# Local attention in six layers: exponentials scaled by the queries' norm, odd heads normalised on GpSimd, another order on TensorE

## The chip, the cores and the metric

The kernel runs on one core of a Trainium2 chip. Its engines run side by side and meet through semaphores: PE (TensorE, matrix products, with PEld for its weight loads), DVE (VectorE), ACT (ScalarE), POOL (GpSimd), and SP, which issues transfers. The metric is the device time of one execution in microseconds, lower is better.

## The reference

A chain of conditional layers and feed-forward layers over `x` of 32 sequences x 128 tokens x 128 features. The change is in the attention of "L2_ffn", which is done six times (`DEPTH`), each time followed by a feed-forward layer:

```python
def attn_layer(x, Wqkv, qs, ksc, Wo):        # x: (32, 128, 128), 16 heads of 64
    q, k, v = heads(x @ Wqkv)
    q = l2norm(q) * qs
    k = l2norm(k) * ksc
    q = q * cos * scale + rotate_half(q) * sin * scale
    k = k * cos / scale + rotate_half(k) * sin / scale
    return heads_back(local_attention(q, k, v)) @ Wo

def local_attention(q, k, v):                # windows of 32: this one and the one before
    sim = einsum('bhwie,bhwje->bhwij', q, k) * 8.0
    sim = where(mask, -finfo.max, sim)
    return einsum('bhwij,bhwje->bhwie', softmax(sim), v)
```

`l2norm(t)` is `t` over its norm within a head. The queries' norm is one number for each token and head, so it can be put on q or on the row of scores.

## The kernel before

`level2_layers` holds the six layers; the other functions stand before and after it and aren't touched. A unit is one sequence and 8 of its 16 heads, so a layer has 32 x 2 = 64 units. Tokens lie on the 128 partitions. The heads of a unit are split by e = 0 (even) and e = 1 (odd): the scores of four heads of 128 x 128 fill one PSUM bank, and `s_ps` has two.

Each engine has its own program. `pipeline(engine, units, period, stages)` writes it: in slot s it calls every stage `(f, g)` of the list for unit s - g, in the order of the list. Eight slots are written out in a loop body (8 times round a layer, less head and tail). The list's order is the order of the engine's queue: what stands behind a waiting instruction waits too. VectorE's slots run one slot number ahead (its list has `rotate` with lag 1 where PE's has `project_k` with lag 0).

What a unit k passes through:

- PE: `project_q` (L1509) and `project_k` (L1512) write q and k, 2 x 512 columns, to `qk_ps`; `project_v` (L1518) writes v to `vy_ps`.
- VectorE: `rotate` (L1860) and `rotate_swapped` (L1866) multiply q and k from PSUM with the rotary tables into `t1` and `t2`. ScalarE: `squares` (L1695) writes `sq` out of `qk_ps`. VectorE: `sums` adds up the squares of a head into `ss` (L1874) and takes the maximum with `tiny` (L1877).
- GpSimd, `norms`: t1 = t1 + t2 (L1798), rs = ss to the power of -1/2 (L1800), qk = t1 x rs for q and k alike (L1805).
- PE: `turn_q` (L1525) and `turn_k` (L1531) transpose four tiles each into `T_ps`; ScalarE copies them with `keep_q` (L1706) and `keep_k` (L1712). As there is one `T_ps`, `turn_k` waits for `keep_q`, and the next `turn_q` for `keep_k`.
- PE, `scores`: a product of the mask (L1541, bf16) and then q by k (L1546) into both banks of `s_ps`; it waits for `kTc` (the copy of k), `p0` and `p1` of the unit before, as the banks are read until then. The tables of q carry the factor -8, and the mask's product is +2^100 where a key may not be seen: `s_ps` holds the negated scores.
- VectorE, `lows`: the minimum of each row and head (L1888), one reduction for each e, each with its own semaphore `low0` or `low1`.
- ScalarE, `exps0` and `exps1` (L1718): four exponentials each, in place, bias `low`, scale -1.0, each with its row sum into `den` (a second instruction, ACTIVATION_READ_ACCUMULATOR).
- VectorE, `normalise0` and `normalise1`: reciprocal of `den` (L1894), then p = s_ps x rec (L1897).
- PE: `turn_p0` and `turn_p1` (L1552), ScalarE `keep_p0` and `keep_p1` (L1732), PE `values` (L1573), ScalarE `keep_o` (L1744), PE `project` (L1584), VectorE `residual` (L1910). `keep_v` (L1701) copies v. `shift` (L1853, L1854), once for two units, prepares the input `xs`.

The orders of the four engines:

```python
pe:   (turn_q,2) (project_q,0) (turn_p1,4) (turn_k,2) (project_k,0)
      (values,4) (turn_p0,3) (project_v,0) (scores,2) (project,4)
act:  (keep_q,2) (keep_p1,4) (exps1,3) (keep_k,2) (keep_o,4) (keep_p0,3)
      (keep_v,0) (squares,0) (exps0,2)
dve:  (normalise0,4) (shift,0) (rotate,1) (normalise1,4) (rotate_swapped,1)
      (lows,3) (sums,1) (residual,5)
pool: norms
```

After 64 units the feed-forward layer follows (`ffn`), on the same engines; its first steps are laced into the last slots (`before`, `after`).

Of the kernel before, what the change touches and what calls it, by code (L numbers as in the profile page):

```python
# [24 lines left out]
P = 128  # L25
# [15 lines left out]
UH = 8  # L41
# [1367 lines left out]
def level2_layers(nc, T, R):  # L1409
# [8 lines left out]
    with ExitStack() as ctx:  # L1418
# [13 lines left out]
        rs = m.sb("rs", [P, 2, 2 * UH])  # L1432
        t1 = m.sb("t1", [P, 2, 2 * UC])
        t2 = m.sb("t2", [P, 2, 2 * UC])
        qk = m.sb("qk", [P, 2, 2 * UC])
        qT = m.sb("qT", [P, 2, 4, P])
        kT = m.sb("kT", [P, 2, 4, P])
        low = m.sb("low", [P, 2, 2, 4])
        den = m.sb("den", [P, 2, 2, 4])
# [31 lines left out]
        names = ("tables", "one", "xs", "qkp", "vp", "vc", "sq", "ss", "ssm", "rs", "t1", "t2", "t12", "qk", "qT",  # L1471
                 "qTc", "kT", "kTc", "scores", "low0", "low1", "ex0", "ex1", "rec0", "rec1", "p0", "p1", "pT0", "pT1",
# [6 lines left out]
        with nc.Block() as block:  # L1479
# [24 lines left out]
            def _(pe):  # L1504
# [16 lines left out]
                def turn_q(k, j, c):  # L1521
                    pe.wait_ge(s_["qk"], at(k))
                    pe.wait_ge(s_["kTc"], at(k - 1))
                    for i in range(4):
                        mm = pe.transpose(T_ps[:, i * P:(i + 1) * P], qk[:, c % 2, i * P:(i + 1) * P], R.ident[:, :])  # L1525
                    mm.then_inc(s_["qT"], 1)

                def turn_k(k, j, c):
                    pe.wait_ge(s_["qTc"], at(k))
                    for i in range(4):  # L1530
                        mm = pe.transpose(T_ps[:, i * P:(i + 1) * P], qk[:, c % 2, UC + i * P:UC + (i + 1) * P],  # L1531
                                          R.ident[:, :])
                    mm.then_inc(s_["kT"], 1)

                def scores(k, j, c):
                    pe.wait_ge(s_["kTc"], at(k))
                    pe.wait_ge(s_["p0"], at(k - 1))
                    pe.wait_ge(s_["p1"], at(k - 1))
# [68 lines left out]
                def spread(l, j):  # L1607
# [5 lines left out]
                    if j == 1:  # L1613
                        pe.wait_ge(s_["p1"], at(l * NU + NU - 1))
# [66 lines left out]
                with pe.Fori(0, DEPTH) as l:  # L1681
                    pe.wait_ge(s_["f_res"], at(l * NG - 1))
                    pipeline(pe, NU, 8, [(turn_q, 2), (project_q, 0), (turn_p1, 4), (turn_k, 2), (project_k, 0),
                                         (values, 4), (turn_p0, 3), (project_v, 0), (scores, 2), (project, 4)],
# [6 lines left out]
            def _(act):  # L1691
# [23 lines left out]
                def exps(k, c, e):  # L1715
                    act.wait_ge(s_[f"low{e}"], at(k))
                    for i in range(4):
                        ins = act.activation(s_ps[:, e, i * P:(i + 1) * P], s_ps[:, e, i * P:(i + 1) * P], ACT.Exp,  # L1718
                                             bias=low[:, c % 2, e, i:i + 1], scale=-1.0,
# [54 lines left out]
                with act.Fori(0, DEPTH) as l:  # L1774
                    pipeline(act, NU, 8, [(keep_q, 2), (keep_p1, 4), (exps1, 3), (keep_k, 2), (keep_o, 4), (keep_p0, 3),
# [1057 lines left out]
```

## Time and profile before

| | us |
|---|---|
| median of 3 runs | 5947.21 |
| lowest, highest | 5918.96, 5953.5 |
| span of the profiled execution | 5933.1 |

The profiled execution's own time isn't listed apart from the runs; its span, from the first to the last instruction, is 14 us under the median. The profile is one execution on the chip. Its first part says how long each engine was busy:

```profile
PE 5194.6 (88%) x43284; PEld 3252.2 (55%) x43296; DVE 3850.6 (65%) x6824; ACT 3367.5 (57%) x9898; POOL 3172.7 (53%) x1509
```

The second part cuts the span into 40 slices and gives busy tenths:

```profile
PE   5994999456599999999999999999999899996864
DVE  2112000752388868886788768886888588856888
ACT  0000000432188957996689759884899499943432
POOL 0000000221388848885688758884888388841018
PEclk9999999668699999999999999999999999997985
```

A digit 9 is 90% or more. The six layers lie in slices 11 to 35, from 1.6 to 5.3 ms; a dip of POOL is a feed-forward layer. A timeline row has the start, the duration, engine and line, output and inputs, the count of instructions merged, and in brackets the idle time ahead of it and what ended it.

### The profile page before, as it was taken

The page shows a single profiled execution, that of the slowest core. Times are in us where ns is not written, and L with a number is a line of the kernel's source. Part 1 is how long each engine was busy: PE and PEld are TensorE (multiplying, and loading weights), DVE is VectorE, ACT ScalarE, POOL GpSimd, SP SyncE. Part 2 cuts the span into 40 slices and gives each one's busy share as a digit, 9 for nine tenths or more (in the row PEclk, how much of TensorE's full clock was granted, in tenths as well). Part 3 has the DMA queues.
Part 4 walks back from the last instruction along what each step waited for, and adds up shares of the span by engine and source line. Part 5 has one row for each costly group of instructions (what it writes and reads, how often), then busy time and mean ns, then how long its engine had stood idle before and what let it go on. Part 6 is the DMA issues. An engine that isn't in the chain of part 4 may idle for free. (4 is left out here: it accounts for less than half of the span.)

```text
span 5933.1 us, 128823 instructions
## 1 busy us (share of the span) xinstructions
PE 5194.6 (88%) x43284; PEld 3252.2 (55%) x43296; DVE 3850.6 (65%) x6824; ACT 3367.5 (57%) x9898; POOL 3172.7 (53%) x1509
## 2 busy tenths in 40 slices
PE   5994999456599999999999999999999899996864
PEld 1331776233366655666566656664666466654532
DVE  2112000752388868886788768886888588856888
ACT  0000000432188957996689759884899499943432
POOL 0000000221388848885688758884888388841018
PEclk9999999668699999999999999999999999997985
DMA  7666554021100000000000000000000000000000
GB/s 227 162 171 156 111 108 101 4 69 47 34 1 0 0 16 5 0 0 16 5 0 0 15 5 0 0 0 20 1 0 0 20 1 0 0 16 13 7 1 14
DMA packets 271956, 199.78 MB, mean 34 GB/s; under 512 B 179032, under 2 KB 254264, under 8 KB 265336
## 3 DMA queue, kind: packets, MB, share of 16 engines
q1 hardware_dynamic: 202073, 119.60, 8.6%
q10 hardware_dynamic: 67487, 71.25, 4.1%
q8 instruction: 229, 3.75, 0.3%
q0 software_dynamic: 2048, 4.20, 0.2%
q14 instruction: 119, 0.97, 0.1%
HBM read 131.83 MB, written 63.16 MB: 33 GB/s over the span
## 5 line engine op out<-in xcount | busy, mean ns | idle before, releaser
L1800 POOL TENSOR_TENSOR rs<-ss,minus_half 128x16 f32<-128x16 f32 x386 | 1127.4, 2921 | 282.3 <-DVE ss L1877 281.5
L1718 ACT ACTIVATE s_ps<-s_ps,low 128x128 f32<-128x128 f32 x3072 | 1050.0, 343 | 81.5 <-DVE low L1888 76.2
L1798 POOL TENSOR_TENSOR t<-t 128x1024 f32<-128x1024 f32 x386 | 909.2, 2356 | 151.9 <-DVE t L1866 151.0
L1805 POOL TENSOR_TENSOR qk<-t,rs 128x1024 f32<-128x1024 f32 x386 | 734.4, 1903 | 60.5 <-POOL rs L1800 23.7
L1718 ACT ACTIVATION_READ_ACCUMULATOR s_ps<-s_ps,low 128x1 f32 x3072 | 641.8, 209 | 0.0
L1888 DVE TENSOR_REDUCE low<-s_ps 128x4 f32<-128x512 f32 x768 | 494.9, 686 | 203.5 <-PE s_ps L1546 203.4
L1860 DVE TENSOR_TENSOR t<-qk_ps,rot 128x1024 f32<-128x1024 f32 x386 | 472.5, 1224 | 162.1 <-PE qk_ps L1512 148.2
L1897 DVE TENSOR_TENSOR p<-s_ps,rec 128x512 f32<-128x512 f32 x768 | 531.0, 691 | 30.5
L1552 PEld LDWEIGHTS pT_ps<-ident,p 128*128 128x128 f32 x3072 | 354.7, 141 | 267.8 <-issue 265.5
L264 PE MATMUL h_ps<-h_x,h_w 9*128 9x512 bf16 x4096 | 439.9, 628 | 69.2 <-DMA h_w<-rows_w1s 54.5
L1732 ACT ACTIVATE pT<-pT_ps 128x512 f32<-128x512 f32 x768 | 459.5, 598 | 64.7 <-PE pT_ps L1552 29.8
L1573 PEld LDWEIGHTS att_oT_ps<-pT,v 128*64 128x64 f32 x6144 | 330.7, 137 | 287.0 <-issue 287.0
L1552 PE MATMUL pT_ps<-ident,p 128*128 128x128 f32 x3072 | 485.0, 281 | 0.8
L1695 ACT ACTIVATE sq<-qk_ps 128x1024 f32<-128x1024 f32 x386 | 395.0, 1023 | 145.9 <-DVE t L1866 114.1
L1874 DVE TENSOR_REDUCE ss<-sq 128x16 f32<-128x1024 f32 x386 | 466.8, 1209 | 4.8 <-ACT sq L1695 4.8
L1866 DVE TENSOR_TENSOR t<-qk_ps,rot 128x1024 f32<-128x1024 f32 x386 | 468.7, 1214 | 0.0
L1584 PE MATMUL vy_ps<-oT,wo 128*128 128x128 f32 x3072 | 447.8, 289 | 4.4 <-ACT oT L1744 4.4
L1573 PE MATMUL att_oT_ps<-pT,v 128*64 128x128 f32 x6144 | 423.7, 280 | 8.8 <-issue 8.8
L1509 PE MATMUL qk_ps<-wqkv,xs 128*128 128x512 f32 x772 | 403.4, 605 | 31.6 <-DVE xs L1854 20.2
L1518 PE MATMUL vy_ps<-wqkv,xs 128*128 128x512 f32 x768 | 400.3, 603 | 29.6 <-ACT v L1701 15.5
L1546 PEld LDWEIGHTS s_ps<-kT,qT 64*128 64x128 f32 x6144 | 407.5, 189 | 9.1
L1546 PE MATMUL s_ps<-kT,qT 64*128 64x128 f32 x6144 | 405.7, 272 | 0.0
(404 smaller groups left out, 8703.6 us busy)
## 6 DMA issues: line engine op xcount, KB each, us to landing
h_x<-rows_xs SPq DMA_DIRECT2D x512, 72.0 KB
rows_hs<-h_parts ACTq DMA_DIRECT2D x88, 384.0 KB, 6.8
z_fm<-rows_hs SPq DMA_DIRECT2D x128, 144.0 KB
x_fm<-rows_hs SPq DMA_DIRECT2D x128, 144.0 KB
wqkv<-in_wqkv SPq DMA_DIRECT2D x7, 1536.0 KB, 6.4
o_w<-rows_exs ACTq DMA_DIRECT2D x512, 18.0 KB
rows_xs<-z_fm ACTq DMA_DIRECT2D x12, 384.0 KB, 5.5
rows_exs<-s_exp ACTq DMA_DIRECT2D x9, 512.0 KB, 6.5
```

Source lines behind the costliest of these rows:

```text
L1546: mm = pe.matmul(s_ps[:, e, i * P:(i + 1) * P], qT[r, c % 2, i, :], kT[r, c % 2, i, :], start=False, stop=True, skip_group_check=True)
L1552: mm = pe.transpose(pT_ps[:, i * P:(i + 1) * P], p[:, c % 2, e, i, :], R.ident[:, :])
L1573: mm = pe.matmul(oT_ps[DH * e:DH * e + DH, i * P:(i + 1) * P], v[:, c % 8, d:d + DH], pT[:, c % 2, e, i, :], start=True, stop=True, skip_g ...
L1718: ins = act.activation(s_ps[:, e, i * P:(i + 1) * P], s_ps[:, e, i * P:(i + 1) * P], ACT.Exp, bias=low[:, c % 2, e, i:i + 1], scale=-1.0, ...
L1798: pool.tensor_tensor(t1[:, i, :], t1[:, i, :], t2[:, i, :], ALU.add).then_inc(s_["t12"], 1)
L1800: pool.tensor_tensor(rs[:, i, :], ss[:, i, :], R.minus_half[:, 0:2 * UH], ALU.pow).then_inc(s_["rs"], 1)
L1805: pool.tensor_tensor(qk[:, i, :].rearrange("p (h d) -> p h d", d=DH), t1[:, i, :].rearrange("p (h d) -> p h d", d=DH), rs[:, i, :].unsquee ...
L1860: dve.tensor_tensor(t1[:, i, :], qk_ps[:, :, :].rearrange("p n c -> p (n c)"), rot[:, 0, :, :, :].rearrange("p a h d -> p (a h d)"), ALU.m ...
L1866: dve.tensor_tensor(t2[:, i, :].rearrange("p (h e d) -> p h e d", e=2, d=DH // 2), swapped(), rot[:, 1, :, :, :].rearrange("p a h (e d) -> ...
L1874: dve.tensor_reduce(ss[:, i, :], sq[:, :].rearrange("p (h d) -> p h d", d=DH), AX.X, ALU.add).then_inc(s_["ss"], 1)
L1888: dve.tensor_reduce(low[:, c % 2, e, :], s_ps[:, e, :].rearrange("p (h k) -> p h k", h=4), AX.X, ALU.min).then_inc(s_[f"low{e}"], 1)
L1897: dve.tensor_tensor(p[:, i, e, :, :], s_ps[:, e, :].rearrange("p (h k) -> p h k", h=4), rec[:, i, e, :].unsqueeze(2).to_broadcast([P, 4, P ...
```

## The change

What it does, in `level2_layers` and the constants:

- The signs are turned: the tables of q carry +8, the mask -2^100, and `s_ps` holds scores.
- q is no longer multiplied with its `rs`: `turn_q` transposes `t1` and waits for `t12` (the addition) alone. Only k is multiplied, into `kn` (half the size). `rs` has four buffers instead of two, as it is used longer.
- `lows` takes the maxima of both e into `top`, waits for them, and writes `low` = -top x rs for all eight heads in one instruction. There is one semaphore `low` for both halves.
- `exps` takes `rs` of its head as scale (a [128,1] operand) instead of the constant -1.0. `exps1` writes to `grown` in SBUF, `exps0` stays in place in PSUM.
- p of the odd heads is made by GpSimd out of `grown` (`normalise1`, before the `norms` of the unit three later); VectorE keeps its reciprocal (`invert1`).
- `scores` waits for `ex1` instead of `p1` of the unit before.
- PE's order: `project_k` between `turn_p1` and `turn_k`, then `project_v`, `values`, `scores`, `turn_p0`, `project`. ScalarE's order: `keep_v` ahead of `keep_o`, then `squares`, `keep_p0`.

```diff
--- before.py
+++ after.py
@@ -1429,13 +1429,15 @@
...
         ss = m.sb("ss", [P, 2, 2 * UH])
-        rs = m.sb("rs", [P, 2, 2 * UH])
+        rs = m.sb("rs", [P, 4, 2 * UH])
...
         t2 = m.sb("t2", [P, 2, 2 * UC])
-        qk = m.sb("qk", [P, 2, 2 * UC])
+        kn = m.sb("kn", [P, 2, UC])
...
         kT = m.sb("kT", [P, 2, 4, P])
+        top = m.sb("att_top", [P, 2, 2, 4])
         low = m.sb("low", [P, 2, 2, 4])
+        grown = m.sb("grown", [P, 2, 4, P])
...
@@ -1519,23 +1521,23 @@
...
                 def turn_q(k, j, c):
-                    pe.wait_ge(s_["qk"], at(k))
+                    pe.wait_ge(s_["t12"], at(k))
...
                     for i in range(4):
-                        mm = pe.transpose(T_ps[:, i * P:(i + 1) * P], qk[:, c % 2, i * P:(i + 1) * P], R.ident[:, :])
+                        mm = pe.transpose(T_ps[:, i * P:(i + 1) * P], t1[:, c % 2, i * P:(i + 1) * P], R.ident[:, :])
...
                 def turn_k(k, j, c):
                     pe.wait_ge(s_["qTc"], at(k))
+                    pe.wait_ge(s_["kn"], at(k))
                     for i in range(4):
-                        mm = pe.transpose(T_ps[:, i * P:(i + 1) * P], qk[:, c % 2, UC + i * P:UC + (i + 1) * P],
-                                          R.ident[:, :])
+                        mm = pe.transpose(T_ps[:, i * P:(i + 1) * P], kn[:, c % 2, i * P:(i + 1) * P], R.ident[:, :])
...
                 def scores(k, j, c):
...
                     pe.wait_ge(s_["p0"], at(k - 1))
-                    pe.wait_ge(s_["p1"], at(k - 1))
+                    pe.wait_ge(s_["ex1"], at(k - 1))
...
@@ -1611,7 +1613,7 @@
...
                     if j == 1:
-                        pe.wait_ge(s_["p1"], at(l * NU + NU - 1))
+                        pe.wait_ge(s_["ex1"], at(l * NU + NU - 1))
...
@@ -1680,8 +1682,8 @@
...
                     pe.wait_ge(s_["f_res"], at(l * NG - 1))
-                    pipeline(pe, NU, 8, [(turn_q, 2), (project_q, 0), (turn_p1, 4), (turn_k, 2), (project_k, 0),
-                                         (values, 4), (turn_p0, 3), (project_v, 0), (scores, 2), (project, 4)],
+                    pipeline(pe, NU, 8, [(turn_q, 2), (project_q, 0), (turn_p1, 4), (project_k, 0), (turn_k, 2),
+                                         (project_v, 0), (values, 4), (scores, 2), (turn_p0, 3), (project, 4)],
...
@@ -1713,10 +1715,14 @@
...
                 def exps(k, c, e):
-                    act.wait_ge(s_[f"low{e}"], at(k))
+                    act.wait_ge(s_["low"], at(k))
+                    if e:
+                        act.wait_ge(s_["p1"], at(k - 2))
                     for i in range(4):
-                        ins = act.activation(s_ps[:, e, i * P:(i + 1) * P], s_ps[:, e, i * P:(i + 1) * P], ACT.Exp,
-                                             bias=low[:, c % 2, e, i:i + 1], scale=-1.0,
+                        h = 2 * i + e
+                        raw = s_ps[:, e, i * P:(i + 1) * P]
+                        ins = act.activation(grown[:, c % 2, i, :] if e else raw, raw, ACT.Exp,
+                                             bias=low[:, c % 2, e, i:i + 1], scale=rs[:, c % 4, h:h + 1],
...
@@ -1772,8 +1778,8 @@
...
                 with act.Fori(0, DEPTH) as l:
-                    pipeline(act, NU, 8, [(keep_q, 2), (keep_p1, 4), (exps1, 3), (keep_k, 2), (keep_o, 4), (keep_p0, 3),
-                                          (keep_v, 0), (squares, 0), (exps0, 2)], k0=l * NU, last=lambda i: after(l, i),
+                    pipeline(act, NU, 8, [(keep_q, 2), (keep_p1, 4), (exps1, 3), (keep_k, 2), (keep_v, 0), (keep_o, 4),
+                                          (squares, 0), (keep_p0, 3), (exps0, 2)], k0=l * NU, last=lambda i: after(l, i),
...
@@ -1797,15 +1803,16 @@
...
                     pool.wait_ge(s_["ssm"], at(k))
-                    pool.tensor_tensor(rs[:, i, :], ss[:, i, :], R.minus_half[:, 0:2 * UH], ALU.pow
+                    pool.wait_ge(s_["ex1"], at(k - 4))
+                    pool.tensor_tensor(rs[:, c % 4, :], ss[:, i, :], R.minus_half[:, 0:2 * UH], ALU.pow
...
                     pool.wait_ge(s_["kT"], at(k - 2))
-                    pool.tensor_tensor(qk[:, i, :].rearrange("p (h d) -> p h d", d=DH),
-                                       t1[:, i, :].rearrange("p (h d) -> p h d", d=DH),
-                                       rs[:, i, :].unsqueeze(2).to_broadcast([P, 2 * UH, DH]), ALU.mult
-                                       ).then_inc(s_["qk"], 1)
+                    pool.tensor_tensor(kn[:, i, :].rearrange("p (h d) -> p h d", d=DH),
+                                       t1[:, i, UC:2 * UC].rearrange("p (h d) -> p h d", d=DH),
+                                       rs[:, c % 4, UH:2 * UH].unsqueeze(2).to_broadcast([P, UH, DH]), ALU.mult
+                                       ).then_inc(s_["kn"], 1)
...
@@ -1817,14 +1824,27 @@
...
 
+                def normalise1(k, c):
+                    i = c % 2
+                    pool.wait_ge(s_["rec1"], at(k))
+                    pool.wait_ge(s_["pT1"], at(k - 2))
+                    pool.tensor_tensor(p[:, i, 1, :, :], grown[:, i, :, :],
+                                       rec[:, i, 1, :].unsqueeze(2).to_broadcast([P, 4, P]), ALU.mult
+                                       ).then_inc(s_["p1"], 1)
+
...
                     for u in range(2, 8):
+                        if u >= 3:
+                            normalise1(l * NU + u - 3, u - 3)
...
                         for u in range(8):
+                            normalise1(l * NU + 5 + i * 8 + u, (u + 5) % 8)
                             norms(l * NU + 8 + i * 8 + u, 8 + i * 8 + u, u)
+                    for u in range(NU - 3, NU):
+                        normalise1(l * NU + u, u % 8)
...
@@ -1856,7 +1876,8 @@
                 def rotate(k, j, c):
...
                     dve.wait_ge(s_["qkp"], at(k))
-                    dve.wait_ge(s_["qk"], at(k - 2))
+                    dve.wait_ge(s_["qT"], at(k - 2))
+                    dve.wait_ge(s_["kn"], at(k - 2))
...
@@ -1885,24 +1906,30 @@
...
                         dve.wait_ge(s_[f"rec{e}"], at(k - 2))
-                        dve.tensor_reduce(low[:, c % 2, e, :], s_ps[:, e, :].rearrange("p (h k) -> p h k", h=4), AX.X,
-                                          ALU.min).then_inc(s_[f"low{e}"], 1)
-
-                def normalise(k, c, e):
+                        ins = dve.tensor_reduce(top[:, c % 2, e, :], s_ps[:, e, :].rearrange("p (h k) -> p h k", h=4),
+                                                AX.X, ALU.max)
+                    ins.then_inc(s_["top"], 1)
+                    dve.wait_ge(s_["top"], at(k))
+                    dve.wait_ge(s_["rs"], at(k))
+                    dve.scalar_tensor_tensor(low[:, c % 2, :, :], top[:, c % 2, :, :], -1.0,
+                                             rs[:, c % 4, 0:UH].rearrange("p (i e) -> p e i", e=2), ALU.mult, ALU.mult
+                                             ).then_inc(s_["low"], 1)
+
+                def normalise0(k, j, c):
                     i = c % 2
-                    dve.wait_ge(s_[f"ex{e}"], at(k))
-                    dve.reciprocal(rec[:, i, e, :], den[:, i, e, :]).then_inc(s_[f"rec{e}"], 1)
-                    dve.wait_ge(s_[f"rec{e}"], at(k))
-                    dve.wait_ge(s_[f"pT{e}"], at(k - 2))
-                    dve.tensor_tensor(p[:, i, e, :, :], s_ps[:, e, :].rearrange("p (h k) -> p h k", h=4),
-                                      rec[:, i, e, :].unsqueeze(2).to_broadcast([P, 4, P]), ALU.mult
-                                      ).then_inc(s_[f"p{e}"], 1)
-
-                def normalise0(k, j, c):
-                    normalise(k, c, 0)
-
-                def normalise1(k, j, c):
-                    normalise(k, c, 1)
+                    dve.wait_ge(s_["ex0"], at(k))
+                    dve.reciprocal(rec[:, i, 0, :], den[:, i, 0, :]).then_inc(s_["rec0"], 1)
+                    dve.wait_ge(s_["rec0"], at(k))
+                    dve.wait_ge(s_["pT0"], at(k - 2))
+                    dve.tensor_tensor(p[:, i, 0, :, :], s_ps[:, 0, :].rearrange("p (h k) -> p h k", h=4),
+                                      rec[:, i, 0, :].unsqueeze(2).to_broadcast([P, 4, P]), ALU.mult
+                                      ).then_inc(s_["p0"], 1)
+
+                def invert1(k, j, c):
+                    i = c % 2
+                    dve.wait_ge(s_["ex1"], at(k))
+                    dve.wait_ge(s_["p1"], at(k - 2))
+                    dve.reciprocal(rec[:, i, 1, :], den[:, i, 1, :]).then_inc(s_["rec1"], 1)
...
@@ -2002,7 +2029,7 @@
...
                 with dve.Fori(0, DEPTH) as l:
-                    pipeline(dve, NU, 8, [(normalise0, 4), (shift, 0), (rotate, 1), (normalise1, 4), (rotate_swapped, 1), (lows, 3),
+                    pipeline(dve, NU, 8, [(normalise0, 4), (shift, 0), (rotate, 1), (invert1, 4), (rotate_swapped, 1), (lows, 3),
...
@@ -2711,7 +2738,7 @@
...
     out = np.empty((S, 2, 2, DH), np.float32)
-    out[:, 0, 0], out[:, 0, 1] = np.cos(freqs) * scale * -8, np.sin(freqs) * scale * sign * -8
+    out[:, 0, 0], out[:, 0, 1] = np.cos(freqs) * scale * 8, np.sin(freqs) * scale * sign * 8
...
@@ -2738,7 +2765,7 @@
...
     b[38:42] = (block[None, :] > w[:, None]) | (block[None, :] < w[:, None] - 1)
-    return np.concatenate([a, a]), np.concatenate([b, b]) * 2.0 ** 100
+    return np.concatenate([a, a]), np.concatenate([b, b]) * -2.0 ** 100
 def constants():
```

## Rows read from the trace of the kernel before

**Rows 1.** Engines by stretch: one slot (us, busy and count by engine, clock).

```profile
2405.44:2413.46 8.02, 8.02 (x66) 5.42 (x65) 6.79 (x12) 7.26 (x24) 7.12 (x4) 1.00 0.00 0
```

**Rows 2.** Timeline, PE, first half of that slot.

```profile
2405.44 0.60 PE L1525 MATMUL T_ps<-ident,qk 128*128 128x128 f32 x4
...
2405.88 1.02 PE L1509 MATMUL qk_ps<-wqkv,xs 128*128 128x512 f32 x2
...
2406.74 0.60 PE L1552 MATMUL pT_ps<-ident,p 128*128 128x128 f32 x4
...
2407.34 0.66 PE L1531 MATMUL T_ps<-ident,qk 128*128 128x128 f32 x4
...
2407.83 1.02 PE L1512 MATMUL qk_ps<-wqkv,xs 128*128 128x512 f32 x2
...
2408.78 1.09 PE L1573 MATMUL att_oT_ps<-pT,v 128*64 128x128 f32 x16
```

**Rows 3.** Timeline, VectorE and GpSimd, one slot.

```profile
2402.82 1.22 DVE L1866 TENSOR_TENSOR t<-qk_ps,rot 128x1024 f32<-128x1024 f32 x1
...
2405.77 1.21 DVE L1874 TENSOR_REDUCE ss<-sq 128x16 f32<-128x1024 f32 x1
...
2407.02 0.17 DVE L1877 TENSOR_TENSOR ss<-ss,tiny 128x16 f32<-128x16 f32 x1
...
2407.27 2.91 POOL L1800 TENSOR_TENSOR rs<-ss,minus_half 128x16 f32<-128x16 f32 x1 [0.76 <-DVE ss L1877]
...
2410.31 1.90 POOL L1805 TENSOR_TENSOR qk<-t,rs 128x1024 f32<-128x1024 f32 x1
...
2412.17 2.36 POOL L1798 TENSOR_TENSOR t<-t 128x1024 f32<-128x1024 f32 x1
```

**Rows 4.** Timeline, ScalarE, the same slot.

```profile
2406.67 0.61 ACT L1706 ACTIVATE qT<-T_ps 128x512 f32<-128x512 f32 x1
...
2407.37 0.60 ACT L1732 ACTIVATE pT<-pT_ps 128x512 f32<-128x512 f32 x1
...
2407.87 0.34 ACT L1718 ACTIVATE s_ps<-s_ps,low 128x128 f32<-128x128 f32 x1
...
2409.23 0.62 ACT L1712 ACTIVATE kT<-T_ps 128x512 f32<-128x512 f32 x1
```

**Rows 5.** Groups by shape: busy us, mean ns of one, idle before.

```profile
L714 ACT ACTIVATE big<-st_ps,magic,sc 128x512 f32<-128x512 f32 x32 | 24.7, 773 | 40.4 <-DVE inv L653 40.4
...
L1753 ACT ACTIVATE ff_sq<-qk_ps 128x512 f32<-128x512 f32 x48 | 28.6, 597 | 0.0
...
L1816 POOL TENSOR_TENSOR ff_diag<-ident,ff_rstd 128x512 f32<-128x512 f32 x48 | 49.9, 1039 | 75.5 <-PE s_ps L1615 74.5
```

**Rows 6.** Timeline, VectorE, around a mask product that waited for p.

```profile
2418.67 0.69 DVE L1897 TENSOR_TENSOR p<-s_ps,rec 128x512 f32<-128x512 f32 x1
...
2420.91 1.29 DVE L1888 TENSOR_REDUCE low<-s_ps 128x4 f32<-128x512 f32 x2 [0.42 <-PE s_ps L1546]
```

**Rows 7.** Timeline, VectorE instructions that began inside one of GpSimd.

```profile
2237.76 2.34 POOL L1798 TENSOR_TENSOR t<-t 128x1024 f32<-128x1024 f32 x1
...
2239.83 0.31 DVE L1877 TENSOR_TENSOR ss<-ss,tiny 128x16 f32<-128x16 f32 x1
...
2243.34 1.90 POOL L1805 TENSOR_TENSOR qk<-t,rs 128x1024 f32<-128x1024 f32 x1 [0.22 <-POOL rs L1800]
...
2243.42 1.97 DVE L1853 SCALAR_TENSOR_TENSOR xs<-z_fm 64x128 f32<-64x128 f32 x1 [3.28 <-issue]
...
2415.29 2.91 POOL L1800 TENSOR_TENSOR rs<-ss,minus_half 128x16 f32<-128x16 f32 x1 [0.76 <-DVE ss L1877]
...
2416.72 0.27 DVE L1853 SCALAR_TENSOR_TENSOR xs<-z_fm 64x128 f32 x1
```

**Rows 8.** Timeline, GpSimd, units 2 and 63 of the first layer.

```profile
1630.59 2.35 POOL L1798 TENSOR_TENSOR t<-t 128x1024 f32<-128x1024 f32 x1 [3.56 <-DVE t L1866]
...
2121.84 2.36 POOL L1798 TENSOR_TENSOR t<-t 128x1024 f32<-128x1024 f32 x1 [0.39 <-DVE t L1866]
```

More of the change, by code:

```diff
@@ L1470, in level2_layers @@
         ffw = m.dma_sem("e_ffw")
-        names = ("tables", "one", "xs", "qkp", "vp", "vc", "sq", "ss", "ssm", "rs", "t1", "t2", "t12", "qk", "qT",
-                 "qTc", "kT", "kTc", "scores", "low0", "low1", "ex0", "ex1", "rec0", "rec1", "p0", "p1", "pT0", "pT1",
+        names = ("tables", "one", "xs", "qkp", "vp", "vc", "sq", "ss", "ssm", "rs", "t1", "t2", "t12", "kn", "qT",
+                 "qTc", "kT", "kTc", "scores", "top", "low", "ex0", "ex1", "rec0", "rec1", "p0", "p1", "pT0", "pT1",
                  "pTc0", "pTc1", "o", "oTc", "proj", "res",
```

## The prediction

> **What bounds the kernel now.** I read the page first, then a table of engines over one stretch, then the timeline of one slot engine by engine, then the groups by shape. The page's busy shares (PE 88%) are an average over stages. The six attention layers fill 3.6 ms of the span, and the change lies in them alone. A layer handles 64 units; in a slot each engine does its stages for several units. GpSimd starts its addition (L1798) for unit 2 at 1630.59 and for unit 63 at 2121.84 [rows 8]: 61 slots in 491.25 us, 8.05 each. In one slot PE is busy 8.02 of 8.02 us [rows 1], and its groups follow each other without a gap [rows 2]: PE bounds the slot. The reader is to see that the groups cost more than their columns: four transposes take 0.44 us up to the next start behind `project` (L1525), but 0.60 ahead of `turn_k`, which waits for ScalarE's copy of q, and 0.49 ahead of `project_k`; a projection takes 0.86 ahead of a transpose and 0.95 ahead of `values`, whose weights are 64 columns wide.
>
> **PE after.** `project_k` now stands between the transposes: `turn_p1` falls from 0.60 to 0.44, `turn_k` from 0.49 to 0.44, `project_k` from 0.95 to 0.86. `project_v` takes over the 0.95 ahead of `values`. The slot becomes 8.02 - 0.16 - 0.05 - 0.09 = 7.72 us. No row shows `values` straight ahead of the mask: between a gain of 0.1 and a loss of 0.17 (what a group of `values` costs over the 0.86 of its columns), so 7.6 to 7.9; I take 7.72. PE alone would give 61 x 6 x 0.33 = 121 us.
>
> **The chain through ScalarE after.** Count from E, the end of the new small product on VectorE (`low` = -top x rs). The exponentials start 0.03 later. Four take 1.36 now (2407.87 to 2409.23, [rows 4]). Each gets a second operand by pointer, the scale. Priced by shapes of 128x512 out of PSUM [rows 5]: two pointers 773 ns, none 597, so 0.09 each; four take 1.72. Then `keep_q` and `keep_p1`, 0.50 each [rows 4], `exps1` 1.72, and `keep_k`, which ends 0.62 after its start: E + 5.09. From a release to the start of the reductions there are 1.55 us by [rows 6] (2419.36 to 2420.91); after ScalarE I take 1.48, as PE starts 0.06 after qT's end in [rows 2, 4]. The next reductions start at E + 6.57. Two take 1.29 [rows 6], 0.04 for the wait on `top`, and the product can be issued at E + 7.90. Undisturbed it takes 0.17, like the 128x16 maximum in [rows 3] (the nearest; an instruction of 8 elements may be below it, a strided read above, 0.1 to 0.3): a slot of 8.09 us. So the wait for both halves (before, `exps0` started after one reduction) and the pointers alone already cost what PE gains: ScalarE's chain is the bound, not PE.
>
> The Trainium skill (ScalarE: Activation LUTs, What ACT_TABLE_LOAD costs) gives about 93 ns for each pointer operand; by it this slot would be 8.13 us.
>
> **The chain through GpSimd after, and the port.** The product reads two tensors in SBUF. [rows 7] shows what happens to such VectorE instructions: the maximum started at 2239.83 inside GpSimd's addition took 0.31 and ended at 2240.14, 0.04 after the addition (2240.10); the shift started at 2243.42 inside the multiplication took 1.97 instead of 0.27 and ended 0.15 after it. Inside the power (L1800) it still takes 0.27 (2416.72): the power doesn't hold it. The rotations, which read PSUM and one tensor in SBUF, keep their duration whatever GpSimd does. Now where is GpSimd when the product is issued? After E: `sums` 1.25 up to the maximum's start, 0.17, 0.08 to wake GpSimd: power at E + 1.50; its next instruction 3.04 later (2407.27 to 2410.31) [rows 3]. `kn` is half of the multiplication of 1.90: between 0.95 and 1.04, the 128x512 product of [rows 5]; I take 1.02, 0.98 up to the next start (they overlap by 0.04). `normalise1` is the same size: 0.98; its input, `rec1`, is ready at E + 4.8 (`exps1` is done by 4.6, the reciprocal follows), before `kn` ends at E + 5.6; the swapped rotation behind it, 1.22 [rows 3], gives t2 to GpSimd by E + 6.14. So the addition for the next unit starts at E + 1.50 + 3.04 + 0.98 + 0.98 = E + 6.50 and ends at E + 8.86. The product, issued at E + 7.90, falls inside it and ends 0.03 after it: the slot is **8.89 us**. It is a closed ring: VectorE's product, sums, power, kn, normalise1, addition, product. Even if ScalarE's pointers cost nothing, the product would be issued at E + 7.2, still inside, and the ring would be as long. Bounds: `kn` and `normalise1` at 0.91 and at 1.04 give 8.75 and 9.01; if they were shorter still, t2 sets the addition's start and 8.53 is the floor.
>
> The Trainium skill has this rule (SBUF — State Buffer, SBUF: two separate sides): a VectorE instruction with two SBUF inputs and a GpSimd instruction that reads SBUF exclude each other, and the loser fully blocks. The trace agrees for addition and multiplication and disagrees for the power, which reads SBUF too.
>
> **What costs nothing.** VectorE loses one product of 0.69 and stays off the ring. The raw q is transposed from `t1`, 4.9 us earlier than now (3.04 and 1.90, [rows 3]). `p1` comes from GpSimd at E + 6.5, two slots ahead of `turn_p1`. The scores no longer wait for `p1`: that removes a stall like the one of [rows 6], which is inside the 8.05. The feed-forward parts are unchanged.
>
> **Sum.** Slot 8.89 - 8.05 = 0.84; 61 x 6 x 0.84 = 307 us. The first two and last three slots of a layer have no such addition and lengthen by between nothing and 0.84: 5 x 6 x 0.4 = 12. Together +319. Against the profiled execution, span 5933, that is 6252; the median of the runs shown is 5947, 14 above the span, so **6266 us**, slower by 5.4%.
>
> **Rivals.**
> 1. The product slips past GpSimd (8 elements; the rows held had 16 and more). Then ScalarE's chain rules, 8.09: 366 x 0.04 = 15, plus 12 at the ends: 5974, no change. For it: the one held maximum was held briefly. Against: every one that met an addition ended after it.
> 2. Faster: the product slips past and the pointer's cost hides behind the accumulator's read. The place is the eight exponentials; ScalarE's chain falls to 7.4 and PE decides at 7.72: 5947 - 121 = 5826. It is faster by 1% from a slot of 7.86, so from a pointer of 0.06 instead of 0.09. Against it: exponentials follow each other at 0.34, their own duration, so what lengthens one spaces them.
> 3. The power holds the port too, as the skill's rule reads. As a mechanism here: the shift, due at E + 2.84 in every second slot, waits until the power ends (E + 4.41, and 0.15), the two rotations of 1.22 and the reciprocal follow, t2 reaches GpSimd near E + 7.56 instead of 6.50, and those slots take 9.95: 366 x 0.5 x 1.06 = 194 more, 6460. Against: [rows 7], 0.27 inside the power. The page is SBUF — State Buffer of the Trainium skill.
> 4. PE, now idle about 1.1 of 8.9 us, is granted 1.2 GHz in stretches: its 7.72 would double there. Ten slots in a hundred would give +240: about 6500. The clock is 1.00 in the slot of [rows 1].
>
> **Chances.** Forecast 0.80, rivals 0.11, 0.05, 0.02, 0.02. The forecast's own range: 8.53 to 9.01 gives 0.48 to 0.96 x 366 = 176 to 351, with 0 to 25 at the ends: 6120 to 6325; with the median's own spread of some 20 us, 6100 to 6345. This leaves out the rivals, 2 in 10. Faster by over 1% 0.05, within 1% (about what a measurement can tell from no change) 0.11, slower 0.84.
>
> **What would show it.** In the changed kernel's timeline: GpSimd's additions 8.9 us apart; the product on VectorE taking near 0.9 to 1 us instead of 0.17 and ending with the addition; ScalarE idle before `exps0` for `low`; exponentials 0.43 apart; PE with a gap of about 1.1 us ahead of the mask; `turn_p1` at 0.44; `kn` and `normalise1` near 1.0. If the product takes 0.17, the forecast falls to rival 1; if the exponentials then stay 0.34 apart, to rival 2. What would make it wrong most easily is a product issued before the addition starts.

## The result and the profile after

| | us |
|---|---|
| before, median of 4 runs | 5948.7 (5919.0 to 5953.5) |
| after, median of 4 runs | 6268.6 (6257.4 to 6275.6) |
| ratio | 1.055, 95% interval 1.053 to 1.058 |
| span of the profiled execution after | 6255.6 |

The changed kernel is slower by 5.5%. The first part of its page:

```profile
PE 5151.8 (82%) x43296; PEld 3243.6 (52%) x43296; DVE 4007.2 (64%) x6824; ACT 3501.4 (56%) x9898; POOL 3222.2 (52%) x1893
...
PEclk9999999578899999999999999999999999998985
```

PE is busy for the same time as before, less 43 us, in a span 322 us longer, and PEclk shows a 9 in every slice of the six layers, as before: it now waits. GpSimd's additions of units 2 and 63 of the first layer, which answer to [rows 8] (timeline, GpSimd):

```profile
1615.05 2.34 POOL L1804 TENSOR_TENSOR t<-t 128x1024 f32<-128x1024 f32 x1 [4.38 <-DVE t L1887]
...
2156.78 2.35 POOL L1804 TENSOR_TENSOR t<-t 128x1024 f32<-128x1024 f32 x1
```

61 slots in 541.73 us are 8.88 each, where there were 8.05. The timeline of all engines over one slot answers to [rows 2] to [rows 4]:

```profile
2504.61 2.35 POOL L1804 TENSOR_TENSOR t<-t 128x1024 f32<-128x1024 f32 x1
...
2504.87 1.06 PE L1586 MATMUL vy_ps<-oT,wo 128*128 128x128 f32 x8
...
2505.76 0.60 PE L1527 MATMUL T_ps<-ident,t 128*128 128x128 f32 x4
2505.82 1.16 DVE L1914 SCALAR_TENSOR_TENSOR low<-att_top,rs 128x8 f32<-128x8 f32 x1
...
2507.01 0.43 ACT L1724 ACTIVATE s_ps<-s_ps,low,rs 128x128 f32<-128x128 f32 x1 [1.35 <-DVE low L1914]
...
2508.40 2.91 POOL L1807 TENSOR_TENSOR rs<-ss,minus_half 128x16 f32<-128x16 f32 x1 [1.44 <-DVE ss L1898]
...
2509.42 0.66 PE L1534 MATMUL T_ps<-ident,kn 128*128 128x128 f32 x4 [0.90 <-ACT qT L1708]
...
2509.73 0.27 DVE L1873 SCALAR_TENSOR_TENSOR xs<-z_fm 64x128 f32 x1
...
2511.44 1.04 POOL L1812 TENSOR_TENSOR kn<-t,rs 128x512 f32<-128x512 f32 x1
...
2511.65 0.18 DVE L1932 RECIPROCAL rec<-den 128x4 f32<-128x4 f32 x1
...
2512.16 0.39 PE L1543 MATMUL s_ps<-mask,maskq 64*128 64x512 bf16 x2 [0.19 <-ACT kT L1714]
...
2512.44 1.04 POOL L1831 TENSOR_TENSOR p<-grown,rec 128x512 f32<-128x512 f32 x1
...
2513.44 2.35 POOL L1804 TENSOR_TENSOR t<-t 128x1024 f32<-128x1024 f32 x1
2513.49 1.29 DVE L1909 TENSOR_REDUCE att_top<-s_ps 128x4 f32<-128x512 f32 x2 [0.55 <-PE s_ps L1548]
...
2514.81 1.00 DVE L1914 SCALAR_TENSOR_TENSOR low<-att_top,rs 128x8 f32<-128x8 f32 x1
```

Read it as the ring. The product starts at 2505.82 inside the addition (2504.61 to 2506.96) and ends at 2506.98, 0.02 after it: 1.16 us for 8 elements. ScalarE has been idle for 1.35 us and starts 0.03 later. GpSimd's power, `kn`, `normalise1` and the next addition follow, and the next product again ends with it, at 2515.81, 8.83 after the first.

The view by line (minimum, median and maximum in ns; who waited, us and times) shows that this is the rule:

```profile
L1914 DVE SCALAR_TENSOR_TENSOR low<-att_top,rs x384: 166/1007/1667, 1616.4 to 5558.0; 128x8 f32<-128x8 f32 x192
...
  ACT s_ps L1724: 466.3, 384
```

ScalarE waited for the product before each of the 384 `exps0`. Of the 384 products, 371 start inside an addition, and each of these ends 0.02 to 0.03 us after it; the other 13 start outside and take 0.17.

### The profile page after: what moved, and what is told of

Read it like the earlier page. It is cut to its first block and busy times, and to the rows that moved or that the text cites. A ratio compares the mean times of both kernels' runs of the same rounds, so it can differ in the third digit from the quotient of the medians.

```text
span 6255.6 us, 131555 instructions
## 1 busy us (share of the span) xinstructions
PE 5151.8 (82%) x43296; PEld 3243.6 (52%) x43296; DVE 4007.2 (64%) x6824; ACT 3501.4 (56%) x9898; POOL 3222.2 (52%) x1893
## 5 line engine op out<-in xcount | busy, mean ns | idle before, releaser
L1724 ACT ACTIVATE s_ps<-s_ps,low,rs 128x128 f32<-128x128 f32 x1536 | 655.8, 427 | 466.3 <-DVE low L1914 466.3
L1724 ACT ACTIVATE grown<-s_ps,low,rs 128x128 f32<-128x128 f32 x1536 | 692.2, 491 | 0.0
L1909 DVE TENSOR_REDUCE att_top<-s_ps 128x4 f32<-128x512 f32 x768 | 494.6, 685 | 226.8 <-PE s_ps L1548 226.2
L1534 PE MATMUL T_ps<-ident,kn 128*128 128x128 f32 x1536 | 252.3, 287 | 320.5 <-ACT qT L1708 320.5
L1534 PEld LDWEIGHTS T_ps<-ident,kn 128*128 128x128 f32 x1536 | 161.9, 141 | 629.6 <-ACT qT L1708 625.9
L1831 POOL TENSOR_TENSOR p<-grown,rec 128x512 f32<-128x512 f32 x384 | 399.3, 1040 | 112.6 <-DVE rec L1932 112.6
L1812 POOL TENSOR_TENSOR kn<-t,rs 128x512 f32<-128x512 f32 x386 | 402.3, 1042 | 60.5 <-POOL rs L1807 23.7
L1586 PE MATMUL vy_ps<-oT,wo 128*128 128x128 f32 x3072 | 411.2, 277 | 4.1 <-ACT oT L1750 4.1
```

The source lines that it names most:

```text
L1534: mm = pe.transpose(T_ps[:, i * P:(i + 1) * P], kn[:, c % 2, i * P:(i + 1) * P], R.ident[:, :])
L1724: ins = act.activation(grown[:, c % 2, i, :] if e else raw, raw, ACT.Exp, bias=low[:, c % 2, e, i:i + 1], scale=rs[:, c % 4, h:h + 1], acc ...
L1909: ins = dve.tensor_reduce(top[:, c % 2, e, :], s_ps[:, e, :].rearrange("p (h k) -> p h k", h=4), AX.X, ALU.max)
```

## The experiments

In every kernel the slot was read as the mean distance between the starts of two additions of GpSimd, over all slots within the layers, some 370. That mean is 8.08 before and 8.89 after. "Product" is the median duration of a product. Times are medians of 2 runs (x2, x3, x4, r1, v3, v4), of 4 (after, x1, x5, v2), of 8 (g1) or of 10 (v1). The ratio is to the kernel before as it was timed together with each kernel, and its medians give the first row.

| kernel | us | ratio to before | slot | product |
|---|---|---|---|---|
| before | 5938.6 to 5948.7 | 1 | 8.08 | none |
| after | 6268.6 | 1.055 (1.053 to 1.058) | 8.89 | 1.01 |
| x1, product with one input | 6277.9 | 1.057 (1.053 to 1.061) | 8.88 | 1.00 |
| x2, x1 and no pointer | 6252.2 | 1.053 | 8.89 | 1.63 |
| x3, no pointer | 6251.9 | 1.053 | 8.89 | 1.63 |
| r1, half of `kn` | 6118.1 | 1.030 | 8.47 | 0.59 |
| x4, orders of before | 6389.1 | 1.076 (1.071 to 1.081) | 9.20 | 0.17 |
| v4, maxima in PSUM, orders of before | 6377.0 | 1.073 (1.070 to 1.076) | 9.18 | 0.17 |
| v1, maxima in PSUM | 5946.7 | 1.001 (1.000 to 1.003) | 8.04 | 0.17 |
| g1, addition waits for the product | 5942.5 | 1.000 (0.999 to 1.002) | 8.03 | 0.17 |
| v3, v1 and no pointer | 5774.7 | 0.972 (0.967 to 0.977) | 7.63 | 0.17 |
| x5, before with the new orders | 5831.2 | 0.982 (0.980 to 0.985) | 7.77 | none |
| v2, v1 and a product for each half | 5795.9 | 0.975 (0.973 to 0.978) | 7.69 | 0.16 |

The slots explain most of the differences: each median less 366 slots leaves 2980 to 3028 us, whichever kernel it is.

**What holds the product: its inputs.** x1 drops `rs` from the product, so that it has one input (and the exponentials subtract an unscaled maximum):

```diff
-dve.scalar_tensor_tensor(low[:, c % 2, :, :], top[:, c % 2, :, :], -1.0, rs[...], ALU.mult, ALU.mult)
+dve.tensor_scalar(low[:, c % 2, :, :], top[:, c % 2, :, :], -1.0, 1.0, ALU.mult, ALU.mult)
```

> The changed kernel with one edit: low is made from top alone by an instruction with one tensor in SBUF; the factor rs is left out of it, so the output isn't the reference's. My theory (the product with two SBUF inputs is held until GpSimd's addition ends, and that closes a ring of 8.9 us): the instruction takes 0.17 instead of 1.0, the ring opens, and the slot falls to ScalarE's chain, 8.09 us, 5,960 to 5,990 us in all. Rival (the product is late for its wait on top or rs, or simply as a third instruction in the chain): nothing changes, 6,269. Second rival (the pointers of the exponentials cost nothing): the slot falls to PE's 7.72, near 5,840.

A miss. Timeline of x1, VectorE and GpSimd:

```profile
2504.36 2.36 POOL L1804 TENSOR_TENSOR t<-t 128x1024 f32<-128x1024 f32 x1
2505.83 0.91 DVE L1914 TENSOR_SCALAR low<-att_top 128x8 f32<-128x8 f32 x1
```

It ends at 2506.74, 0.02 after the addition, as the product did. So "two inputs in SBUF" isn't the whole condition: this instruction with one input and its output in SBUF is held too. The Trainium skill (SBUF — State Buffer, Who interferes with whom) names this other case: a `tensor_scalar` can run in a mode that uses two ports, when its operands meet that mode's conditions, and then contends with GpSimd. The trace shows the hold; whether such a mode was in use it doesn't show. x2 adds to x1 what x3 does below, so it met the same hold.

> As x1_low_one_input, and the scale of the exponentials is the constant 1.0 again; the queries' norm is left out altogether, so the output isn't the reference's. Theory (0.09 us for each pointer, 8 of them in ScalarE's chain): ScalarE's chain falls to 7.4, PE becomes the bound with 7.72 a slot, 5,830 to 5,860 us, and the exponentials follow each other at 0.34 instead of 0.43. Rival (the pointers are hidden behind the accumulator's read): the same time as x1_low_one_input.

A miss for the same reason.

v1 leaves the product as it is and writes the maxima to PSUM, where a part of the tile `oT` is free at that time, so that the product has one input in PSUM and one in SBUF. `values` waits for the product of the next unit before it overwrites them.

```diff
-ins = dve.tensor_reduce(top[:, c % 2, e, :], s_ps[...], AX.X, ALU.max)
+ins = dve.tensor_reduce(oT_ps[:, 4 * e:4 * e + 4], s_ps[...], AX.X, ALU.max)
```

> The changed kernel, complete, with top written to eight columns of a PSUM bank that is free at that moment (att_oT_ps, between keep_o and the next values) instead of SBUF, so that the product reads one tensor in SBUF and one in PSUM. x1 took the second SBUF input away and the instruction was still held (1.0 us), so either the port theory is wrong or an instruction from SBUF to SBUF with a constant takes the shared port too. Port theory: with an operand in PSUM the product takes 0.17; the slot is ScalarE's chain, 6.51 us from low's end to the next reductions (changed kernel's timeline) + 1.33 + 0.17 = 8.01, so 6,268 - 366 x 0.87 = 5,950 (5,935 to 5,980). Rival (the third instruction waits for something else at that place, whatever it reads): the product stays near 1.0 us and the time near 6,270.

The timeline of v1, the same two lines:

```profile
2502.28 2.37 POOL L1805 TENSOR_TENSOR t<-t 128x1024 f32<-128x1024 f32 x1
2503.49 0.17 DVE L1916 SCALAR_TENSOR_TENSOR low<-att_oT_ps,rs 128x8 f32<-128x8 f32 x1
...
2510.29 2.37 POOL L1805 TENSOR_TENSOR t<-t 128x1024 f32<-128x1024 f32 x1
```

The product takes 0.17 us in the midst of the addition, as in all of the 372 slots where it starts inside one, and the 322 us are gone. g1 removes the same loss without touching the product: GpSimd waits until it has ended.

```diff
 pool.wait_ge(s_["t2"], at(k))
+pool.wait_ge(s_["low"], at(k - 2))
 pool.tensor_tensor(t1[:, i, :], t1[:, i, :], t2[:, i, :], ALU.add)
```

> The changed kernel complete, and GpSimd's addition waits in each slot until VectorE's product of that slot has ended. Theory: the product then runs with GpSimd idle (0.17 us, not 1.0), its end is set by ScalarE's chain, and the slot is that of v1, 8.0 to 8.1 us: 5945 to 5985 us. The addition, the power and the two multiplications that follow start about 1.5 us later than in v1 but have 8.01 - (2.36 + 3.04 + 2 x 1.0) = 0.6 us left in a slot. Rival: GpSimd's queue is itself the ring (its four operations with the waits between them), and a later addition pushes the rest of the slot back: 6268 us or more.

The timeline of g1, the same lines:

```profile
2500.28 0.17 DVE L1915 SCALAR_TENSOR_TENSOR low<-att_top,rs 128x8 f32<-128x8 f32 x1
2500.53 2.36 POOL L1805 TENSOR_TENSOR t<-t 128x1024 f32<-128x1024 f32 x1 [0.37 <-DVE low L1915]
...
2501.61 1.30 DVE L1899 TENSOR_TENSOR ss<-ss,tiny 128x16 f32<-128x16 f32 x1
...
2503.07 2.91 POOL L1808 TENSOR_TENSOR rs<-ss,minus_half 128x16 f32<-128x16 f32 x1 [0.19 <-DVE ss L1899]
```

GpSimd idles 0.37 us ahead of the addition. The hold itself hasn't gone: it has moved to the next instruction with two inputs in SBUF, the maximum with `tiny`, which now starts inside the addition in 380 of 386 cases, takes 1.30 us here (1.36 in the median) instead of 0.17 and ends at 2502.91, 0.02 after the addition. The power waits for it, but ScalarE doesn't, and the time isn't longer for it. The time is 2.5 us under the expected range, less than the runs of g1 differ (5923.8 to 5949.5). Two different repairs, 5946.7 and 5942.5 us, come out alike: the meeting of these two instructions is worth the whole loss, and what is left is a slot of 8.0.

**Is it GpSimd's ring?** x3 replaces the pointer to the norm in the scale of the exponentials with the constant 1.0 (the norm is left out), which shortens ScalarE's chain. r1 makes `kn` for four of eight heads (the other half is zero), which shortens the ring.

```diff
-bias=low[:, c % 2, e, i:i + 1], scale=rs[:, c % 4, h:h + 1],
+bias=low[:, c % 2, e, i:i + 1], scale=1.0,
```

> The changed kernel with the constant scale 1.0 in the exponentials, low as it is (two SBUF inputs); the norm is left out of the exponent, so the output isn't the reference's. Ring theory: ScalarE isn't on the ring, so the slot stays 8.88 and the time 6,260 to 6,275 us; the product is only issued 0.7 us earlier and held 0.7 us longer. Rival (ScalarE's chain with its pointers is what sets the slot): 8 x 0.09 x 366 = 260 us less, near 6,010.

> The changed kernel with kn made for four of the unit's eight heads only; the keys of the other four stay zero, so the output isn't the reference's. Ring theory (GpSimd's length counts one for one while it is off the page's list of busy engines, 52%): the instruction falls from 1.04 to about 0.6, the slot by 0.43, the time by 366 x 0.43 = 160 us to 6,110. The product is issued at the same distance and held 0.4 shorter. Rival (the product's delay is of its own length): 6,269.

The slots are as the ring theory says. r1 is 8 us above the time expected. x3, at 6251.9, is 8 us under its range, but its slot is unchanged at 8.89. In x3 (view by line) the product is issued earlier and just held for longer:

```profile
L1914 DVE SCALAR_TENSOR_TENSOR low<-att_top,rs x384: 166/1633/2361, 1624.0 to 5556.9; 128x8 f32<-128x8 f32 x192
```

In r1 `kn` takes 0.61 us instead of 1.04; GpSimd's next instruction starts 0.57 after it instead of 1.00, and the slot falls by 0.42. Time taken off the ring counts in full (0.42 of 0.43 us), and the 0.7 us taken off ScalarE's chain in x3 leave the slot as it is.

**What the pointers cost when nothing hides them.** v3 is x3's edit on v1.

> As v1 (largest scores in PSUM, so that the product is not held), and the exponentials take the constant 1.0 for their scale instead of the pointer to the queries' norm, which leaves the norm out of them. Theory: in v1 the slot of 8.01 us is ScalarE's chain, eight exponentials of it at 0.43 us each where 0.34 us was seen without the pointer. Without it the chain is 8.01 - 8 x 0.09 = 7.3 us, below TensorE's own 7.6 to 7.7, so the slot is TensorE's and the time 5946 - 390 x 0.35 to 0.4, that is 5785 to 5815 us. Rival: the pointer costs nothing where it stands and the slot of v1 is something else's; then 5947 us.

The groups of v3 and after, form by form:

```profile
L1725 ACT ACTIVATE s_ps<-s_ps,low 128x128 f32<-128x128 f32 x1536 | 520.9, 339 | 130.2 <-DVE low L1916 129.7
```

```profile
L1724 ACT ACTIVATE s_ps<-s_ps,low,rs 128x128 f32<-128x128 f32 x1536 | 655.8, 427 | 466.3 <-DVE low L1914 466.3
```

427 - 339 = 88 ns for a pointer. The same edit brings 172 us here (5946.7 to 5774.7) and at most 17 in x3: the kernel before took 5940.6 in the runs beside x3 and 5948.7 in those beside the changed kernel, so half of the 17 is a difference between the two measurements. The time came out 10 us below the range expected. So in v1 ScalarE's chain was the bound, and here it is PE.

**What the orders are worth.** x4 gives the changed kernel the orders of PE and ScalarE that the kernel before has; the lines show PE's.

```diff
-(turn_p1, 4), (project_k, 0), (turn_k, 2), (project_v, 0), (values, 4), (scores, 2), (turn_p0, 3), (project, 4)
+(turn_p1, 4), (turn_k, 2), (project_k, 0), (values, 4), (turn_p0, 3), (project_v, 0), (scores, 2), (project, 4)
```

> The changed kernel with PE's and ScalarE's stages in the order of the kernel before. Ring theory: neither order is on the ring; PE needs 8.0 instead of 7.7 a slot, still under 8.88: 6,260 to 6,290 us. Rival (the new order costs the time, by a wait that it brings): the time falls towards 5,975 or lower.

A miss: 6389 us, and the product is held in 7 of 384 cases only. Timeline of x4, all engines:

```profile
2500.54 2.36 POOL L1804 TENSOR_TENSOR t<-t 128x1024 f32<-128x1024 f32 x1
...
2503.06 0.17 DVE L1914 SCALAR_TENSOR_TENSOR low<-att_top,rs 128x8 f32<-128x8 f32 x1
...
2505.67 0.66 PE L1534 MATMUL T_ps<-ident,kn 128*128 128x128 f32 x4 [1.16 <-ACT qT L1708]
...
2507.12 1.09 PE L1575 MATMUL att_oT_ps<-pT,v 128*64 128x128 f32 x16
...
2508.14 0.66 PE L1554 MATMUL pT_ps<-ident,p 128*128 128x128 f32 x4
...
2509.59 0.39 PE L1543 MATMUL s_ps<-mask,maskq 64*128 64x512 bf16 x2
...
2510.80 1.16 PE L1586 MATMUL vy_ps<-oT,wo 128*128 128x128 f32 x8
2511.01 1.29 DVE L1909 TENSOR_REDUCE att_top<-s_ps 128x4 f32<-128x512 f32 x2 [1.36 <-PE s_ps L1548]
...
2511.80 0.60 PE L1527 MATMUL T_ps<-ident,t 128*128 128x128 f32 x4
...
2512.34 0.17 DVE L1914 SCALAR_TENSOR_TENSOR low<-att_top,rs 128x8 f32<-128x8 f32 x1
```

`turn_k` waits for ScalarE's copy of q, which stands behind `exps0`, and so behind the product: 2.44 us after the product's end (2503.23). After it PE does `project_k`, `values`, `turn_p0` and `project_v` ahead of the mask, 3.92 us; reductions 1.42 later, product after 1.33, and 0.17: 9.28 us. The expectation had looked at the ring alone and left this chain out. The product comes 0.16 after the addition has ended, and so runs free. v4 asks whether it is a chain or a hold in another place: it is x4's order with the maxima in PSUM, where nothing is held.

> As v1, with the orders of work on TensorE and ScalarE that the kernel before has. Theory: the 9.20 us slot of the changed kernel with the old orders was ScalarE's and TensorE's chain (the values wait for the product, and the next unit's projection of k, its transpose, the second turn of p and the values stand before the mask) and not the held product, so it stays: 6370 to 6400 us. Rival: it was the product's hold in another place; then it falls to 6100 us or under, as v1 fell by 320 us against the changed kernel.

It stays at 6377, with a product of at most 168 ns. So it is the chain. With the single product, the new orders are worth 430 us (v4 to v1). x5 takes the new orders alone, on the kernel before, complete.

> The kernel before with PE's and ScalarE's stages in the new order and nothing else; complete. By the PE step: the slot falls from 8.05 to 7.7, as q's copy no longer delays turn_k and one projection less stands ahead of a product with half-size weights: 5,820 to 5,850 us. ScalarE's chain is 7.1 there (one reduction before exps0, no pointer), GpSimd's sum 7.3. Rival (values straight ahead of the mask costs what it saves, or scores, which still waits for p1 of VectorE, comes too late): 5,930 to 5,970.

5831 us: worth 107 us there. Timeline of x5, PE, `values` and the mask of one slot and `values` of the next:

```profile
2502.39 1.09 PE L1573 MATMUL att_oT_ps<-pT,v 128*64 128x128 f32 x16
2503.41 0.39 PE L1541 MATMUL s_ps<-mask,maskq 64*128 64x512 bf16 x2
...
2510.00 0.32 PE L1573 MATMUL att_oT_ps<-pT,v 128*64 128x128 f32 x1
```

An undisturbed slot is 7.61. The mean is 7.77. x5 keeps a wait that the change takes out: `scores` waits for VectorE's p of the odd heads. The first line is that wait in the view of waits of x5; the second is the mask's wait in v2 below, where `scores` waits for `ex1` instead:

```profile
PE s_ps L1541 <- DVE p L1897: 51.7, 66, 1.9
```

```profile
PE s_ps L1542 <- ACT kT L1715: 24.6, 65, 1.1
```

The numbers are us in total, times, and the longest. 51.7 us over 366 slots are 0.14 of the 0.16 that the mean lies above 7.61. In the kernel before, with the old orders, the same wait for p took 15.3 us in 38 times: the rival that x5's expectation names is real, but costs less than the orders bring.

**A version that beats both.** v2 is v1 with a product for each half, so that `exps0` starts after one reduction, as in the kernel before. It computes all of it.

```diff
-ins.then_inc(s_["top"], 1)
-dve.wait_ge(s_["top"], at(k))
-dve.scalar_tensor_tensor(low[:, c % 2, :, :], oT_ps[:, 0:8]..., -1.0, rs[...], ...).then_inc(s_["low"], 1)
+    .then_inc(s_[f"top{e}"], 1)
+    dve.wait_ge(s_[f"top{e}"], at(k))
+    dve.scalar_tensor_tensor(low[:, c % 2, e, :], oT_ps[:, 4 * e:4 * e + 4], -1.0,
+                             rs[:, c % 4, e:UH:2], ...).then_inc(s_[f"low{e}"], 1)
```

> v1_top_in_psum with the product made for each half right behind its reduction, and a semaphore for each half, as the kernel before had it; complete. If ScalarE's chain sets the slot of v1_top_in_psum, it shortens by 0.6 to 7.4 and PE's groups (0.44 + 0.86 + 0.44 + 0.86 + 0.50 + 0.96 + 1.03 + 0.23 + 0.99 + 0.49 + 0.89 = 7.69 by the changed kernel's timeline) become the bound, with GpSimd's 7.4 just under it: 7.7 to 7.8 a slot, 5,835 to 5,870 us, faster than both kernels. Rival (GpSimd's ring stays closed through the maximum with tiny, which has two SBUF inputs, or through shift): 8.0 or more, not faster than the kernel before.

5795.9 us, 2.5% under the kernel before and 39 us below the range expected. The timeline, VectorE and GpSimd:

```profile
2501.27 2.36 POOL L1805 TENSOR_TENSOR t<-t 128x1024 f32<-128x1024 f32 x1
2501.45 0.16 DVE L1915 SCALAR_TENSOR_TENSOR low<-att_oT_ps,rs 128x4 f32<-128x4 f32 x1
...
2502.25 0.16 DVE L1915 SCALAR_TENSOR_TENSOR low<-att_oT_ps,rs 128x4 f32<-128x4 f32 x1
...
2508.88 2.36 POOL L1805 TENSOR_TENSOR t<-t 128x1024 f32<-128x1024 f32 x1
```

The first product starts 0.18 into the addition and isn't held. The second one is off the chain, since `exps1` comes behind `exps0` and two copies. The two additions shown are 7.61 apart, PE's undisturbed slot.

The account of the change: the orders alone -107 us (before to x5); the single product with its wait for both halves, the pointers and the rest +115 (x5 to v1; taken from v1 one by one, the single product is worth 151 us, v1 to v2, and the pointers 172, v1 to v3, as each alone brings the slot down to PE's); the hold +322 (v1 to after).

## Why the prediction was right, and where it was off

- **The ring.** Predicted slot 8.89, measured 8.88 between units 2 and 63, 8.89 over all. Its terms: `kn` and `normalise1` 1.00 each up to the next start where 0.98 was taken (they take 1.04, the upper bound, as in [rows 5]); power to `kn` 3.04; product end to power 1.42 instead of 1.50 (`sums` starts 0.07 before the held product has ended). That makes 8.83 in the slot shown, 0.06 under the prediction. In two slots of every eight it is 9.00 (additions at 1615.05, 1624.05 and 1633.05), which the prediction didn't foresee, and which brings the mean back to 8.88. The body of the loop is eight slots long, so these may be the slots where it starts again; no run tests that. The ring and not ScalarE's chain sets the slot: x3 and r1 show it. That 6266 lies within 3 us of the measured 6268.6 is in part luck: slots 0.06 shorter than predicted are made up for by those of 9.00 and by longer ends.
- **The hold.** Predicted 0.9 to 1 us, ending 0.03 after the addition; measured 1.01, ending 0.02 after. The mechanism is shown by v1 and g1. The stated condition, two inputs in SBUF, was enough against GpSimd's addition, and isn't necessary (x1). The same kind of hold takes the maximum with `tiny` in g1.
- **The power does not hold VectorE.** Rival 3 falls: the shift at 2509.73 takes 0.27 inside the power of 2508.40, as in [rows 7]. The product itself was never issued inside a power, so for it this is open.
- **ScalarE's chain**, predicted 8.09, is 8.01 in a slot of v1. The prediction's own terms add up to 7.90 + 0.17 = 8.07, so 8.09 is 0.02 too long, and the 8.13 beside it as well; the forecast of 8.89 uses neither. As to the rest, the two copies took 0.48 each instead of 0.50, from `keep_k`'s start to the product it was 3.35 us instead of 3.43, and the eight exponentials took 3.50 instead of 3.44. So rival 1, 5974 us, would have come out near the 5947 of v1. The pointer at 0.09 was right (0.088).
- **PE alone**, predicted 7.72, is 7.61. The step that failed is the list of groups: in the old order `project` stands behind `scores` and takes 1.00 up to `turn_q` (2510.80 to 2511.80 in x4), in the new one behind `turn_p0`, and takes 0.89 (2504.87 to 2505.76). The prediction priced `turn_p1`, `turn_k` and `project_k` and left this 0.11 out. `values` ahead of the mask cost 1.02 in x5, as ahead of `turn_p0` in x4. None of this showed, as PE wasn't the bound.
- **PE's gap**, predicted at 1.1 us ahead of the mask, is 1.09 in all, but 0.90 of it stands ahead of `turn_k`, for the copy of q. The prediction followed the chain from ScalarE to the mask only, and left out that `turn_k` needs `keep_q` in it.
- **The ends** of the layers: the span grew by 322.5; 366 slots by 0.83 are 304, so the ends took 18 where 12 was taken.
- **Rival 2** needed the product to slip past GpSimd and the pointers to cost nothing, and neither was so. v3, which has neither cost, takes 5775 us where 5826 was worked out, mainly because PE's slot is 7.61 and not 7.72 (366 x 0.11 = 40).
- **Rival 4** fell: the granted clock is 0.98 over 2000 to 2500 us (0.99 before), and PEclk stays at 9 in the six layers.

What stays open: which mode the one-input product of x1 ran in, and a part of why v2 is 35 us faster than x5 (22 us by the spans of the profiled executions). Within the layers PE waits 51.7 us for p and 6.8 for the copy of q ahead of `turn_k` in x5, and 24.6 for the copy of k and 14.9 for that of q in v2: 19 us less. No run changes this wait alone.

## What to carry to other kernels

A VectorE instruction of a few elements on the critical chain can cost nearly the length of a GpSimd instruction (up to 1.67 us for the product, and 2.36 in x3): before adding one, look at where its inputs and its output lie and what GpSimd is doing at the time it will be issued. An input in PSUM, or a wait that puts the GpSimd instruction behind it, takes the loss away; the second can move the hold to the next such instruction, as in g1, which costs nothing only while that one is off the chain. Once such a hold has closed a ring, savings on other engines bring little or nothing until it is opened (the same edit gave at most 17 us before and 172 after), and the order of work on the engine that seems idle decides which stages stand in the chain.

## What the runs showed of the hardware that was not expected

- A `tensor_scalar` of 128x8 from SBUF to SBUF, 0.17 us when free, took 1.00 in the median and up to 1.66 while GpSimd added two tensors of SBUF. Not every short instruction in SBUF is held: the reciprocal of 128x4 at 2511.65 in the changed kernel takes 0.18 us inside `kn`.
- The same 128x8 product with one input in PSUM took 165 to 168 ns in all 384 cases (v1), though 372 of them start inside GpSimd's addition.
- A group of matmuls costs more or less by what it stands behind: the eight of `project` took 1.00 us up to the next start behind `scores` and 0.89 behind transposes. No run asked why.
